# Two selective scans and two dense layers of a fused kernel, run as one stage by batch rows

## The reference

```
x = x + L2_attn_a(layernorm(x))     # selective scan, one branch
x = x + L2_ffn(layernorm(x))        # dense layer
x = x + L2_attn_b(layernorm(x))     # selective scan, two branches, y = y1 - y2
x = x + L2_ffn(layernorm(x))        # the same dense layer again

# a selective scan, for 256 inner features d and 16 states n, along the time t of a row
u = silu(conv4(x_part)); delta = softplus(dt_in @ dt_proj + bias)
h[t,d,n] = h[t-1,d,n] * exp(delta[t,d] * A[d,n]) + delta[t,d] * u[t,d] * B[t,n]
y[t,d]   = sum_n h[t,d,n] * C[t,n] + u[t,d] * D[d];   out = (y * silu(z)) @ out_proj

# the dense layer, hidden width 512
h = silu(x @ w1 * s1) * (x @ w2 * s2)
h = gelu(h @ h1 * sh1); h = gelu(h @ h2 * sh2);  out = h @ w3 * s3
```

## Time and profile before

| what | value |
|---|---|
| runs | 3507.25 us median of 3 (3505.64 to 3509.61) |
| profiled execution | 3502.91 us, its span 3501.2 us |
| layers 9 to 12 | 1746.6 to 2761.2 us of the span |
| scan loops, first scan to last | 1776.2 to 1983.2 and 2181.6 to 2588.6 us |
| dense rows, from one residual addition to the next | 37.7 us |

### The profile page before, as it was taken

One profiled execution on the slowest core, in us unless ns is written; L12 is line 12 of the kernel. 1 busy time (PEld: TensorE's weight loads), 2 busy tenths in 40 slices (PEclk: granted clock), 3 DMA queues, 4 the chain that ended last, 5 costly groups with the idle time before them and its releaser, 6 DMA issues. The chain is left out here.

```text
span 3501.2 us, 58499 instructions
## 1 busy us (share of the span) xinstructions
PE 3038.1 (87%) x21850; PEld 1758.3 (50%) x21857; DVE 2206.0 (63%) x5868; ACT 1676.9 (48%) x3791; POOL 1032.1 (29%) x453
## 2 busy tenths in 40 slices
PE   8888899997888888898987799777679899989998
PEld 3333344445777777643444443444444344556447
DVE  5777445546666666656579701999960267963991
ACT  3555523424444444335266524666642365753762
POOL 1111100000000000000079500999950204950990
PEclk8999999997555555599988799688889899999999
DMA  5434331120000000020343101333310200231124
GB/s 151 109 97 94 95 95 49 46 84 31 3 3 3 3 3 3 3 71 29 111 153 109 42 0 34 108 112 108 109 42 0 88 1 24 97 145 72 72 97 180
DMA packets 113498, 234.32 MB, mean 67 GB/s; under 512 B 13760, under 2 KB 50752, under 8 KB 104768
## 3 DMA queue, kind: packets, MB, share of 16 engines
q1 hardware_dynamic: 113216, 230.59, 20.6%
HBM read 185.71 MB, written 44.83 MB: 66 GB/s over the span
## 5 line engine op out<-in xcount | busy, mean ns | idle before, releaser
L1249 PE MATMUL psum<-h_ring,h_parts 128*128 128x4 bf16 (+2 forms) x12288 | 417.6, 170 | 121.2 <-ACT h_ring L1337 121.2
L1249 PEld LDWEIGHTS psum<-h_ring,h_parts 128*128 128x128 bf16 x12288 | 371.8, 105 | 171.2 <-ACT h_ring L1337 144.9
L2170 POOL TENSOR_TENSOR s_dbu<-s_du,s_bb 128x1024 f32<-128x1024 f32 x190 | 443.5, 2363 | 35.8 <-DMA s_bb<-s_wide 35.8
L2258 DVE TENSOR_TENSOR_SCAN s_hh<-psum,s_dbu 128x512 f32<-128x512 f32 x384 | 443.8, 1206 | 9.6 <-ACT psum L2095 5.0
L2095 ACT ACTIVATE psum<-s_delta,s_decay 128x512 f32<-128x512 f32 x384 | 261.5, 688 | 214.4 <-DVE s_hh L2258 213.0
L1957 PE MATMUL psum<-w_c,s_term 128*128 128x128 f32 x1536 | 275.9, 333 | 74.2 <-POOL s_term L2177 62.2
L1337 ACT ACTIVATE h_ring<-h_pre 128x16 f32<-128x16 f32 x1024 | 168.5, 211 | 357.0 <-DVE h_pre L1399 357.0
L1957 PEld LDWEIGHTS psum<-w_c,s_term 128*128 128x128 f32 x1536 | 234.4, 175 | 166.6 <-POOL s_term L2177 72.0
L901 POOL MEMSET r_weights<- 128x512 f32 x4 | 2.1, 524 | 929.7 <-POOLq L1222 660.4
L910 DVE TENSOR_TENSOR f_hid<-f_gate,psum 128x512 f32<-128x512 f32 x184 | 126.5, 688 | 204.8 <-PE psum L836 197.9
L1399 DVE TENSOR_REDUCE h_pre<-psum 128x16 f32<-128x48 f32 x1024 | 165.2, 203 | 140.9 <-PE psum L1249 140.9
(11 more groups left out here) (494 smaller groups left out, 6172.2 us busy)
## 6 DMA issues: line engine op xcount, KB each, us to landing
s_bb<-s_wide SPq DMA_DIRECT2D x192, 256.0 KB, 3.4
x_spill<-x_flip SPq DMA_DIRECT2D x28, 1024.0 KB, 3.9
f_share<-f_wide SPq DMA_DIRECT2D x208, 128.0 KB, 3.0
s_cc<-s_wide SPq DMA_DIRECT2D x60, 256.0 KB, 3.3
a_ks<-a_spread SPq DMA_DIRECT2D x96, 128.0 KB, 3.3
a_qs<-a_spread SPq DMA_DIRECT2D x96, 128.0 KB, 4.0
x_spare<-x_spill SPq DMA_DIRECT2D x4, 2048.0 KB, 7.7
x_raw<-x_spill SPq DMA_DIRECT2D x4, 2048.0 KB, 7.7
```

The costliest lines, as they stand in the source:

```text
L1249: mm = nc.tensor.matmul(columns_of(s // BLOCK, grp)[:, s % BLOCK, 0:3 - part, cols], parts[:, part, GROUP * grp + p, :], upper[:, (s - 1) ...
L2170: nc.gpsimd.tensor_tensor(dbu[:, s % D_RING], du[:, t % 2], both(bb[:, s % B_RING, :]), ALU.mult).then_inc(dbu_ready, 1)
L2258: nc.vector.tensor_tensor_scan(hh[:, s % 4, half, :], DECAYS[i % 3], dbu[:, s % D_RING, half, :], 0.0, ALU.mult, ALU.add).then_inc(scan_do ...
```

## The change

One stage, `scans_and_dense`, takes the place of four. It has 12 turns (jobs 0 to 3 are the rows of scan one, 4 to 7 those of scan two, with two turns each), 192 steps and 384 slots without a stop between them. Three tables of slots place the rest: `DENSE_AT` and `PAUSES` say in which slots six of the eight dense rows run (51 slots each, with gaps of 4), and `BACK_AT` where the end of a finished row goes. The last two dense rows (rows 2 and 3 of the second dense layer) follow after the loop, in the manner of the old dense stage.

- All 19 products and sums of a dense row in the loop go through the one bank SPARE, one after another, as do the two `turn_back` rounds of a row. The rates' second half now goes to PICK_C instead of SPARE.
- Gate, h1 and h2 values 0 to 2 are copied out of SPARE scaled (`keep_scaled`); when value 3 is ready, `bend` loads the table, applies Silu or Gelu to all four, and loads the old table.
- The norm of a later row is done on that row alone, in PRE (second scan) or SPARE (dense): Square and a copy to `normed` on ScalarE, Ln and Exp, and the multiplication on GpSimd (`scale_two`, `scale_dense`).
- In the odd turns from 3 on, norm, convolution, projection and rates of the next row follow each other in the slots 2 to 24, and GpSimd makes `du` at step 13 instead of 7. Convolution products go by twos to a slot instead of one by one.
- The ring of `dbu` has 5 entries instead of 6; `s_yt` is gone, and `s_y` takes its part. The table of weights "l3a" is loaded after this stage, not at the start of the program.

The core of the diff:

```diff
-def dense_ffn(g):
-def selective_scan(g, pack, ranks, tables):
+def scans_and_dense(g):
+    JOBS, TURNS = 2 * CHUNKS, 3 * CHUNKS
+    D_RING, D_AHEAD = 5, 3
+    HIDDEN, ROW = 6, 51
+    DENSE_AT = (46, 101, 160, 215, 270, 321)
+    PAUSES = ((25,), (2, 31), (41,), (48,), (), (6,))
+    BACK_AT = (39, 71, 103, 136, 201, 263, 327)
+    def place(d, o):
+        return DENSE_AT[d] + o + 4 * sum(p <= o for p in PAUSES[d])
...
+    starts = ({"centre": 0, "mean": 2, "out": 48} | {("gate", m): 6 + 2 * m for m in range(HID)} | {("up", m): 14 + 2 * i for i, m in enumerate(ORDER)}
+              | {("h1", m): 22 + 3 * m for m in range(HID)} | {("h2", m): 35 + 3 * m for m in range(HID)})
...
+                def hidden(d, name, m, part):        # TensorE: two products a slot, four a round
+                    source = low if name == "h1" else high
+                    if part == 0:
+                        open_spare((d, (name, m)))
+                    for i in ((0, 1), (2, 3))[part]:
+                        k = ORDER[i]
+                        if name == "h2" and i and m == 0:
+                            pe.wait_ge(act_done, 6 * d + i)
+                        mm = nc.tensor.matmul(SPARE, ffn[name][...], source[:, k, :], start=(i == 0), stop=(i == HID - 1))
...
+                def bend(d, name, home, function, scale, done, table):     # ScalarE
+                    nc.scalar.preload_act_table_set(table)
+                    act.wait_ge(spare_ready, spare_at[(d, (name, HID - 1))] + 1)
+                    nc.scalar.activation(home[:, HID - 1, :], SPARE, function, scale=scale[:, HID - 1:HID]).then_inc(spare_free, 1)
+                    for m in range(HID - 1):
+                        nc.scalar.activation(home[:, m, :], home[:, m, :], function).then_inc(done, 1)
+                    nc.scalar.preload_act_table_set("natural_log_exp_and_others")
...
+                    if o == 13:
+                        bend(d, "gate", high, ACT.Silu, ffn["s1"], gated, "silu_and_others")
+                    if o == 33:
+                        bend(d, "h1", high, ACT.Gelu, ffn["sh1"], act_done, "gelu_and_others")
+                    if o == 46:
+                        bend(d, "h2", low, ACT.Gelu, ffn["sh2"], act_done, "gelu_and_others")
...
+                def scale_dense(d):                  # GpSimd
+                    pool.wait_ge(d_rstd, d + 1)
+                    x = fixed(g.normed, d % CHUNKS)
+                    nc.gpsimd.tensor_tensor(x, x, d_scale, ALU.mult).then_inc(d_normed, 1)
...
+                tail_dense(0)
+                tail_dense(1)
...
-        place_weights(("c32", "l2a", "l3a"), sb)
+        place_weights(("c32", "l2a"), sb)
```

More of the change, by code:

```diff
@@ new lines, in mean, with project_out @@
+                def mean(j):
+                    open_pre(("mean", j))
+                    pe.wait_ge(p_squared, j - CHUNKS + 1)
+                    nc.tensor.matmul(PRE, g.mean_of, p_scale, start=True, stop=True).then_inc(pre_ready, 1)
+                def project_out(j):
+                    open_pre(("out", j))
+                    pe.wait_ge(spare_free, spare_at[("back", j, 1)] + 1)
+                    for half in range(2):
+                        mm = nc.tensor.matmul(PRE, layer(j)["out"][:, half * P:(half + 1) * P], y[:, half, :],
+                                              start=(half == 0), stop=(half == 1))
+                    mm.then_inc(pre_ready, 1)
@@ new lines, in turn_back @@
+                def turn_back(j, half):
+                    open_spare(("back", j, half))
+                    pe.wait_ge(through_ready, 2 if j < CHUNKS else 4)
+                    pe.wait_ge(y_kept, 2 * j + 2)
+                    nc.tensor.matmul(SPARE, through[:, j // CHUNKS, half, :], u[:, j % U_RING, half, :],
+                                     start=True, stop=True, skip_group_check=True)
+                    for q in range(QT):
+                        mm = nc.tensor.matmul(SPARE[:, q * P:(q + 1) * P], y[:, half, q * P:(q + 1) * P], g.ident, is_transpose=True,
+                                              start=False, stop=True, skip_group_check=True)
+                    mm.then_inc(spare_ready, 1)
@@ L1992, in _ @@
                     if t < TURNS:
-                        slot(t, 2 * n)
+                        chain(t, 2 * n)
                     if s >= 3 and s != STEPS:
@@ L2143, in _ @@
+                for s in range(3):
+                    decays(s, 0)
+                    decays(s, 1)
+                nc.scalar.preload_act_table_set("silu_and_others")
+                for half in range(2):
+                    first_silu(1, half)
+                nc.scalar.preload_act_table_set("natural_log_exp_and_others")
                 for s in range(STEPS):
                     t, n = divmod(s, N)
-                    if s + 1 < STEPS and s + 1 > made:
+                    if s + 1 < STEPS and s + 1 > 2:
```

1005 lines of the change are left out of this document (591 added, 414 removed).

## The result

The changed kernel takes 3383.3 us in the median of four runs (3378.3 to 3388.0), the kernel before 3506.8 (3505.6 to 3509.6): ratio 0.9647, 95% interval 0.963 to 0.9663. It is faster by 123.5 us; 203 were forecast, and the time lies above the range of 3258 to 3368. The profiled execution took 3385.07 us, its span 3383.4.

A forecast was written before the change was run, and what follows sets the result against it. GpSimd was taken to bound the loop, VectorE 3% behind. Head 29.6, loop 691 (625 + 21 + 10 + 25 + 10) and tail 91 made 811.6 against 1014.6 us; forecast time 3304 us, range 3258 to 3368.

The forecast's parts named there:

- the base: Loop: GpSimd's 614.5 us plus 12.5 for ten norm multiplications, less some 2 for one ramp-up, gives 625.
- the price of the dense rows: Loop: 21 for TensorE's turns, 10 for its steps, 25 for bends, 10 for the clock, 7.5 for GpSimd norms.
- The head: Stretch before the first scan: unchanged at 29.6 us.
- the tail: After the last scan: projection end 12.3 us, two dense rows at 37.7, norm products and last sum 3; 91 in all.
- the next stage: Attention after this stage, reading table l3a, now loaded later: cost 0, at worst 4 us.
- rival C: Bends in the loop: table switches cost more than the load, 2.76 us for each of 18; +50, time 3354, chance 0.02.
- rivals B and C: Loop: B, TensorE bounds at clock 0.78, time 3353; C, dearer table switches, 3354. With similar losses, chance 0.24 together.
- Cost 0 by itself: Loop: 30 gate products and sums on VectorE, 19.5 us, leave it level with GpSimd and add no time.
- half of the waits are absorbed: Loop: of 49 us VectorE waits behind 18 bends, half is hidden by TensorE's stretched turns and GpSimd; +25, range 0 to 49.
- TensorE's four turns: Loop turns 2, 4, 7 and 9: TensorE's work exceeds GpSimd's 51 to 52 us by 4.6, 4.6, 2.5 and 9.4; +21.
- a sign beforehand: Loop turns with little dense work (0, 1, 10): longer than 56 us would show the forecast wrong.
- Rival D: Loop: the single bank SPARE locks the engines together over 114 rounds, 2.5 us each, 285 us; time 3589, chance 0.03.

The follow-up runs named there:

- e4_no_dense: Changed kernel without the six dense rows in the loop, the two in the tail kept: loop 666.0 us, ratio to the kernel before 0.9347.
- e18: Changed kernel without the six dense rows in the loop, with six dbu tiles and five B tiles: loop 666.2 us, ratio to the kernel before 0.9366.
- e2: Changed kernel with two of the four products per h1 or h2 chunk left out in the loop's dense rows: loop 741.9 us, ratio 0.9580.
- e8: Changed kernel with dense products alternating between two PSUM banks, the decays' middle tile moved to SBUF: loop 844.1 us, ratio 0.9826.
- e7_ring5: Changed kernel with five decay tiles instead of three, two in SBUF, made further ahead, and five B tiles: loop 847.2 us, ratio 0.9859.
- e21: Changed kernel with norms first, fused bend functions, bursts in odd slots, six dbu and five B tiles, six terms on GpSimd: loop 754.6 us, ratio 0.9599.

## Why the prediction was wrong

The loop was put at 691 us and took 774.9. Of the 84 us between, 48.5 are missing in the base and 35.5 in the price of the dense rows.

**Right.** The head (29.7), the tail (90.4 against 91), the next stage: its first product reads table l3a at 2651.79, 5.3 us after the tail's end, where it was 6.6 (2767.76 - 2761.2).

```profile
2651.79 1.96 PE L2670 MATMUL psum<-normed,w_l3a 128*128 128x512 f32 x4 [0.54 <-DVE normed L137]
```

A multiplication of 512 columns on GpSimd took 1.28 us, the line through two other sizes gave 1.25. The clock of the loop is 0.92, above the 0.9 named. A decay starts 0.02 us behind a table load (2295.62 and 2295.64 above), and all 82 loads of the loop take 1.28 us, so the drain of rival C is not there in the new loads either. The times of rivals B and C (3353 and 3354) lie nearer than the forecast, but that is luck: TensorE is idle for 129 us of the loop at a clock of 0.92, and there is no drain.

**Failed: the base of the loop.** The forecast took GpSimd's 614.5 plus its norms, 617 without those of the dense rows, and put what comes to VectorE at "Cost 0 by itself". Measured without dense rows: 666.0. VectorE's work and waits were 587.9 and 26.6 us in the two loops of before (197.18 + 390.72 of 614.5); they are 604.0 and 62.0 there. 16 us of work and 35 us of waits had been left out or set at nothing, and with VectorE 3% behind GpSimd there was no slack for either. Of the work, the taps of the second layer make 7.6 us: one multiplication that took 1.21 us between the loops before, with GpSimd idle, and that now stands behind GpSimd's products (last section). Two multiplications into `s_through` make 3.7, where they took 0.6.

Of the waits, scans waited 31.9 us for decays instead of 5.0, and row ends make 15.9 instead of 1.1. The 31.9 can be followed one by one. VectorE has three scans in hand, 3.75 us, or more when a term lies between them; a scan waits for what the gap in the decays, plus 0.69 for the next decay, is longer than that. A gap of 3.68 gives some 0.65, and this is seen five times in the loops before as well. The forecast took the earlier trace rows as its model, where half a term more lay in hand and the wait was 0.27. In the new loop:

- Softplus groups cost 7.9 us instead of 0.5. Behind the five of eleven that delay a scan only the three scans were in hand. The second function of a group also waits for the rates' second product (4.9 us in ten groups), which now goes to PICK_C and there waits for VectorE's last term. The forecast had no price for this move.
- Silu groups cost 11.4 us instead of 4.5. The two functions in one group make a gap of 4.63 (1.6 us, twice), and in turns 5, 7 and 9 the group stands where only two scans are in hand (1.62 each).
- Copies that wait for TensorE cost 12.6: 11.0 of it in turns 5, 7 and 9, behind the same copy of the convolution as in the chain of four engines above.

The longest of the Softplus group, in turn 3 of e4_no_dense (L1878 is the product into PICK_C):

```profile
2002.91 0.69 ACT L2217 ACTIVATE s_delta<-psum,w_l2b 128x512 f32<-128x512 f32 x1 [1.66 <-PE psum L1878]
...
2005.64 2.34 DVE L2550 TENSOR_TENSOR_SCAN s_hh<-psum,s_dbu 128x512 f32<-128x512 f32 x2 [2.64 <-ACT psum L2161]
```

The ring of dbu tiles is not the reason (e18).

**Failed: half of the waits are absorbed.** The dense rows were put at 73.5 us (21 + 10 + 25 + 10 and 7.5 of norms); they cost 109.0. The waits behind the bends were sized about right before they were halved: 49 us were forecast, 44.5 measured. That is in part luck in the split, for only seven of the 18 bends keep the decays apart for the 4.9 us of the forecast; in the others ScalarE also stands inside or beside the bend, for a product or for Softplus. Taking half of them, because they lie in turns that TensorE stretches or under GpSimd, was wrong: the loads alone are worth 29.8, and they add to TensorE's 33.1 without a rest. The remaining 46 hold the 21 of work that VectorE does for the dense rows, which the forecast cost at 0 with its slack gone, and 25 more of waits. These 25 are a remainder; no run takes them apart.

**Failed: TensorE's four turns.** The forecast lets the dense work stretch turns 2, 4, 7 and 9 by 2.5 to 9.4 us. Against e4_no_dense every turn from 1 on is longer: turns 3 to 9 by 9.0 to 15.3 us, turns 1, 2, 10 and 11 by 5.6 to 7.5. Turn 9 takes 70.8 instead of 60 to 63. The forecast named a sign beforehand, turns 0, 1 and 10 longer than 56 us, and it came (61.1, 65.1, 58.2); turns 0 and 1 are over 56 without any dense row too (63.3 and 59.5), so there it is first of all the base that shows. TensorE's busy share is 83%, not 85. It is the busiest engine in turns 2 to 7 and in turn 9, yet idle in each for some 4 us or more (busy for 56.5 of 60.4 us in turn 2, 65.2 of 70.8 in turn 9), and 66 us less of its busy time in e2 gave 33. So its work counts in single steps, where VectorE stands for a spread, a product or a row end; that it bounds a turn as a whole is not shown.

**Rival D** was weighed as a price per round of one bank and given 0.03. Its chain (a copy waits for TensorE, decays stand behind the copy, scans behind the decays) is in the traces, but of the 82.4 us that scans waited for decays only some 18 do not stand behind table loads, against its 285. TensorE's products of `up` waited 23.6 us for SPARE to be emptied, 1.0 in each of 24 rounds, more than the 0.5 that the forecast named as a sign of being wrong. The copies of the projection, which the forecast took to be on time before, had waited there too: 4.4 us in three times in the first loop. What a second bank would give stays open (e8).

## What to carry to other kernels

Where two engines are level to a few per cent, reckon a merged loop as the work of the one that the others wait for, plus its waits; in this loop no part of either was hidden under the other engine's bound. A wait behind a burst is read from the work in hand where the burst will stand, not from one burst of the old loop. Take away one cause and then two: gains that add say series, and then small reorderings pay too (here 18 us for moving bursts by one slot, fusing functions and moving norms). An engine that has become idle is where work can go, even the slower one: two terms a turn moved to GpSimd gained 11.5 us, although each takes it 2.36 us and VectorE 1.20.

## What the runs showed of the hardware

VectorE and GpSimd hinder each other when VectorE reads both inputs from SBUF. In e7_ring5 140 scans of this kind that began while GpSimd was in a product took 2.30 us in the mean, up to 3.4; 14 that began while it was idle took 1.20. Scans with one input in PSUM took 1.20 in both cases. The ten norm multiplications on VectorE took 1.49 and 1.90 us where one with an input in PSUM takes 0.69. The Trainium skill (SBUF — State Buffer, Who interferes with whom) says that a VectorE instruction with two SBUF inputs contends with a GpSimd instruction that reads SBUF; the traces agree, and show it for the scan. With one of the three PSUM banks of decays given away (e8) VectorE is busy 117 us longer and the loop takes 69 more.

The wait can outlast one product of GpSimd. The multiplication of the second layer's taps has both inputs in SBUF. Alone, between the loops before, and then in e4_no_dense beside four products that follow each other:

```profile
2156.35 1.21 DVE L2201 TENSOR_TENSOR w_l2b<-w_l2b 128x1024 f32<-128x1024 f32 x1
...
1824.18 9.27 POOL L2420 TENSOR_TENSOR s_dbu<-s_du,s_bb 128x1024 f32<-128x1024 f32 x4
1826.90 7.63 DVE L2464 TENSOR_TENSOR w_l2b<-w_l2b 128x1024 f32<-128x1024 f32 x1
```

It ended 1.08 us after the last of them. In e21, beside six products in a row, it took 13.27 us and ended 1.08 after the sixth. In the changed kernel it began 0.23 us ahead of a product: it took 1.20, and the product 3.17 instead of 2.37. A multiplication of this kind is best placed where GpSimd is idle.
